# Loads of x in five pieces, new batch order and filler counts at both ends of attention, and an earlier weight split in the experts

## The chip, the core and the metric

The kernel runs on one core of one Trainium2 chip. The metric is the device time of one execution in microseconds (us); lower is better. Three executions of the kernel before took 906.54, 910.2 and 913.91 us, so the median is 910.2 us.

## What is computed

Two layers, each an attention over a context and then a mixture of experts, on x of 8 batches of 256 tokens of width 256, all in float32:

```python
x = x + tanh(g_xattn[0]) * L0_xattn(layernorm(x), ctx, ctx, ...)   # 16 heads of 16, softmax, output projection
x = x + tanh(g_ffn[0])   * L0_ffn(layernorm(x), ...)               # 8 experts, top 2, gelu, 256 -> 1024 -> 256, biases
x = x + tanh(g_xattn[1]) * L1_xattn(layernorm(x), ctx, mask, ...)  # the same shape, no mask applied
x = x + tanh(g_ffn[1])   * L1_ffn(layernorm(x), ...)               # top 2 of 8 by softmax; 7 experts with relu and a
                                                                   # capacity of 256 tokens each, the 8th passes x on
```

## The kernel before

The program is six phases, one after the other, with all engines meeting between them: attention, routing and experts of layer 0 (called L0), then the same of layer 1 (L1). The engines are named as in the profile: PE (TensorE), DVE (VectorE), ACT (ScalarE), POOL (GpSimd), SP (the queue that issues most DMAs). Within a phase each engine runs a list of steps written out by hand, and semaphores tie the lists together. A step that waits holds up everything behind it on its engine.

**Attention.** The unit is a batch b of 256 tokens. In float32 every projection is three matmuls of split operands: an operand is kept as a rounded high part (made by ACT for weights and x, by POOL for the context) and a low part (made by DVE, `weight_low`, `inputs_low`; for the context by POOL). A batch goes through `moments` and `normalise_rows` (layernorm; the two small steps between them, `rows_scale`, are POOL's), `x_transpose`, `queries`, `keys` and `values` on PE into one shared PSUM bank `ps_lin`, then eight `head_scores` whose row maxima DVE takes (`take_maxima`, 16 halves a batch), `max_transpose`, copies of queries, keys and maxima into slots by small DMAs on SP (`queries_to_slots`, `keys_to_slots`, `maxima_to_slots`), four chunks of `scores`, exponentials on ACT (`probabilities`) and `weigh_values`, `turn_heads`, `o_transpose`, `out_project`, and at last the layernorm and logits for the router. Batches overlap: a loop over b = 1 to 4 holds the steady state, and the first and last batches have lists of their own. `values(0)` needs `wv` split, and the bank `ps_lin` emptied by `keys(0)`. POOL also writes ones into `v` (`value_ones`), which `values(0)` waits for on DVE.

x is loaded by two DMAs, the first batch alone and then the other seven together, behind all four weights, and the wait for the second stands in `moments(1)`:

```python
def moments(b):
    if b < 2:
        dve.wait_ge(x_ld[b], 16)
```

**Fillers.** `fill_first(n)` and `fill_last(n)` are n transposes of the identity into a PSUM bank that nothing reads. They stand in PE's list where PE is expected to wait. Before the change there are 62 of them at the start of an attention phase and 42 at its end, in each layer.

**Experts.** The unit is a block of 256 gathered tokens with the weights of one expert: 23 blocks in L0, 7 in L1. PE runs `first_product(b + 1)` and then `second_product(b)`. The first product of a block needs its tokens turned (`turn`), split into high (`inputs_high` on ACT) and low (`inputs_low` on DVE), and its first weights split (`w1_high` on ACT, `w1_low` on DVE). For block b + 1 this is done among the four steps (jp = 0 to 3) in which ACT applies the activation of block b (`hidden`) and DVE splits the result (`hidden_parts`). `second_product` fills both halves (q = 0, 1) of one PSUM bank; DVE takes it out (`output`), in L0 ACT weighs it (`weigh`), and POOL adds it to the tokens in DRAM with two indirect DMAs (`add_to_tokens`), which first wait until those of the block before have landed:

```python
pool.wait_ge(y_ready, b + 1)
if b:
    pool.wait_ge(y_out[(b - 1) % 2], loaded(b - 1, QT))
```

## Time and profile before

| | |
|---|---|
| median of three runs | 910.2 us |
| lowest, highest | 906.54, 913.91 us |
| the profiled execution: its own time | 913.08 us |
| its span, from the first to the last instruction | 911.3 us |
| PE, DVE, ACT, POOL busy in the span | 791.0, 634.0, 467.3, 396.3 us |
| granted TensorE clock, mean | 0.901 |

The profiled execution took 2.9 us more than the median, and 1.8 us of its time lie outside the span. Times in the rows are microseconds from the start of the span unless marked ns. L0 attention runs from 4.2 to about 235 us, its experts from about 260 to 547; L1 attention from about 552 to 777, its experts from about 805 to the end.

### The profile page before, as it was taken

The numbers are of one execution on the slowest core, as the hardware profiler recorded it, in microseconds if no ns is written. First come the engines' busy times: TensorE is split into PE (matmuls) and PEld (weight loads), VectorE is DVE, ScalarE is ACT, GpSimd is POOL, SyncE is SP. The second block draws the span as 40 slices with busy tenths as digits, with TensorE's granted clock in tenths as the row PEclk, the third lists the DMA queues.
The fourth block names the chain that finished last, engine by engine and source line by source line (L and its number), as shares of the span: only waits on it lengthen the run. The fifth ranks groups of instructions, "written<-read, shape, count | busy, mean of one in ns | idle before, by whom it ended". The sixth has DMA issues, their size and how long they took to land. (4 is left out here: it accounts for less than half of the span.)

```text
span 911.3 us, 17723 instructions
## 1 busy us (share of the span) xinstructions
PE 791.0 (87%) x6936; PEld 662.9 (73%) x6936; DVE 634.0 (70%) x1207; ACT 467.3 (51%) x696; POOL 396.3 (43%) x374
## 2 busy tenths in 40 slices
PE   5889999998438999999999975999999998348995
PEld 5566677656338999999999974666676656338995
DVE  3667776642658999999999932677776743758882
ACT  3256666444036766666667632166666542335540
POOL 4534453110134677777777443544543110232652
PEclk9779999888859999999999997699999988658998
DMA  7112111021166777887777527112111020775742
GB/s 218 37 37 60 51 50 44 8 74 39 49 235 241 220 243 236 242 237 240 238 240 239 139 30 209 40 38 62 51 51 40 13 83 25 203 185 195 231 85 32
DMA packets 57139, 113.74 MB, mean 125 GB/s; under 512 B 14176, under 2 KB 43360, under 8 KB 49376
## 3 DMA queue, kind: packets, MB, share of 16 engines
q0 software_dynamic: 20256, 69.43, 27.1%
q1 hardware_dynamic: 36800, 43.18, 15.6%
q8 instruction: 55, 0.90, 0.4%
q14 instruction: 28, 0.23, 0.1%
HBM read 85.17 MB, written 18.75 MB: 114 GB/s over the span
## 5 line engine op out<-in xcount | busy, mean ns | idle before, releaser
L563 DVE TENSOR_REDUCE mx_a<-ps_max_a 128x2 f32<-128x512 f32 x256 | 164.4, 685 | 67.8 <-PE ps_max_a L826 65.3
L73 PE MATMUL ps_h_e<-xe_t_e,w_e 128*128 128x256 f32 x480 | 141.3, 294 | 9.7 <-DVE xe_t_e L1659 9.7
L435 ACT ACTIVATE prob_a<-ps_st_a 128x2048 f32<-128x2048 f32 x64 | 120.1, 1876 | 54.8 <-PE ps_st_a L846 45.4
L75 PE MATMUL ps_h_e<-xe_t_e,w_e 128*128 128x256 f32 x480 | 138.0, 287 | 0.0
L74 PE MATMUL ps_h_e<-xe_t_e,w_e 128*128 128x256 f32 x480 | 138.0, 287 | 0.0
L73 PE MATMUL ps_y_e<-w_e,h_e 128*128 128x256 f32 x480 | 132.8, 277 | 0.0
L75 PE MATMUL ps_y_e<-w_e,h_e 128*128 128x256 f32 x480 | 132.7, 276 | 0.0
L74 PE MATMUL ps_y_e<-w_e,h_e 128*128 128x256 f32 x480 | 132.7, 276 | 0.0
L73 PEld LDWEIGHTS ps_h_e<-xe_t_e,w_e 128*128 128x128 f32 x480 | 95.6, 199 | 10.9 <-DVE xe_t_e L1659 10.9
L1503 POOL DMA_INDIRECT xe_e<-normalised_weighted,token_of x60 | 78.5, 1309 | 46.8 <-POOLq L61 19.8
L312 POOL TENSOR_SCALAR r_var_eps_a<-r_mean_var_a 128x2 f32<-128x2 f32 x16 | 3.7, 229 | 216.3 <-DVE r_mean_var_a L590 216.3
L74 PEld LDWEIGHTS ps_h_e<-xe_t_e,w_e 128*128 128x128 f32 x480 | 94.3, 196 | 0.0
L75 PEld LDWEIGHTS ps_h_e<-xe_t_e,w_e 128*128 128x128 f32 x480 | 93.9, 196 | 0.0
L1525 POOL DMA_INDIRECT x<-y_e,token_of x46 | 78.5, 1706 | 34.2 <-ACT y_e L1579 18.6
L75 PEld LDWEIGHTS ps_y_e<-w_e,h_e 128*128 128x128 f32 x480 | 90.1, 188 | 0.0
L73 PEld LDWEIGHTS ps_y_e<-w_e,h_e 128*128 128x128 f32 x480 | 90.1, 188 | 0.0
L74 PEld LDWEIGHTS ps_y_e<-w_e,h_e 128*128 128x128 f32 x480 | 90.1, 188 | 0.0
L846 PE MATMUL ps_st_a<-q_s_a,k_s_a 17*128 17x256 f32 x1024 | 84.1, 424 | 4.9 <-DMA q_s_a<-m_t_a 4.3
L1634 DVE TENSOR_TENSOR h_e<-hid_e,h_e 128x512 fp32r<-128x512 f32 x120 | 84.2, 702 | 4.1
L826 PE MATMUL ps_max_a<-k_r_a,q_r_a 32*128 32x512 f32 x256 | 81.6, 561 | 4.1 <-DVE mx_a L563 1.9
L1570 ACT ACTIVATE hid_e<-ps_h_e,b_e 128x256 f32<-128x256 f32 x184 | 77.5, 482 | 6.8 <-PE ps_h_e L75 6.8
L1552 ACT ACTIVATE w_e<-w_raw_w 128x1024 fp32r<-128x1024 f32 x60 | 64.4, 1076 | 28.9 <-PEq L61 28.9
(210 smaller groups left out, 1746.8 us busy)
## 6 DMA issues: line engine op xcount, KB each, us to landing
w_raw_w<-L_w SPq DMA_DIRECT2D x14, 1024.0 KB
ctx_raw_a<-ctx_t SPq DMA_DIRECT2D x16, 256.0 KB, 5.3
k_s_a<-k_c_a SPq DMA_DIRECT2D x128, 32.0 KB, 2.0
q_s_a<-q_c_a SPq DMA_DIRECT2D x128, 32.0 KB, 2.0
normalised_weighted<-xr SPq DMA_DIRECT2D x16, 256.0 KB, 2.3
x_sb<-x SPq DMA_DIRECT2D x2, 1792.0 KB
x<-x_sb SPq DMA_DIRECT2D x8, 256.0 KB, 2.5
out<-x_sb SPq DMA_DIRECT2D x8, 256.0 KB, 2.5
```

Source lines behind the costliest of these rows:

```text
L73: pe.matmul(out, lhs[0], rhs[0], start=start, stop=False)
L74: pe.matmul(out, lhs[1], rhs[0], start=False, stop=False)
L75: return pe.matmul(out, lhs[0], rhs[1], start=False, stop=stop)
L435: act.activation(prob[n % 2][:, :, :, :], ps_st[:, :, :, :], ACT.Exp, scale=HD ** -0.5).then_inc(prob_ready, 1)
L563: dve.tensor_reduce(mx[:, q, h + 2 * j:h + 2 * j + 2], ps_max[j][:, :, :], AX.X, ALU.max).then_inc(max_done, 1)
L826: pe.matmul(ps_max[j][:, :, :], q_r[b % 2][r:r + 32, c, q * P:(q + 1) * P], k_r[b % 2][r:r + 32, c, :, :], start=True, stop=True).then_inc ...
L846: ins = pe.matmul(ps_st[:, g, kt, :], k_s[b % 3][rows, c, kt * P:(kt + 1) * P], q_s[b % 3][rows, c, :], start=True, stop=True)
L1503: pool.indirect_dma_start(out=xe[b % 2][:, q, :], out_offset=None, in_=dram["xw"], in_offset=bass.IndirectOffsetOnAxis(ap=shared["token_of ...
L1525: pool.indirect_dma_start(out=dram["out" if layer else "x1"], out_offset=bass.IndirectOffsetOnAxis(ap=shared["token_of"][:, t:t + 1], axis=0),
L1552: act.activation(w1[b % 2][0][:, k, :, :], w1_raw[b % 2][:, k * F:(k + 1) * F].rearrange("p (j f) -> p j f", j=FC), ACT.Copy).then_inc(w1_ ...
L1570: ins = act.activation(hid[jp % 2][:, j, :], ps_h[jp % RB][:, j, :], ACT.Gelu, bias=b1[b % 2][:, 2 * jp + j:2 * jp + j + 1])
L1634: dve.tensor_tensor(h[b % 2][1][:, js, :], hid[jp % 2][:, :, :], h[b % 2][0][:, js, :].bitcast(F32), ALU.subtract).then_inc(h_ready, 1)
```

## The change

Attention: x comes in five DMAs (batches 0 to 3 one each, then batches 4 to 7 together), set among the weights and context on SP's queue; `moments(b)` waits for its own piece. The order of the steps of the first and last batches is changed on all engines, and the filler counts rise from 62 to 86 at the start and from 42 to 75 at the end, in each layer. Experts: the first weights of blocks 0 and 1 are both split ahead of `inputs_high(0)` and `inputs_low(0)`; block 1's tokens are turned after the first quarter of `first_product(0)` and not the third, and split at jp = 1 and not 3; an unused Gelu on ACT in L0 stands ahead of the first block; and in the last block each half goes out by itself, the second half in the other PSUM bank.

```diff
@@ -222,19 +223,31 @@
                     sp.dma_start(q_s[b % 3][HD:P:32, c, :], m_t[c * HG:c * HG + HG, :]).then_inc(m_ld, 16)
 
             src = (dram["x1"][0:N, :] if layer else dram["x"]).rearrange("(t p) d -> p t d", p=P)
-            sp.dma_start(x[:, 0:QT, :], src[:, 0:QT, :]).then_inc(x_ld[0], 16)
-            sp.dma_start(w_raw["wq"][:, :, :], w3["wq"]).then_inc(wq_ld, 16)
+
+            def load_x(i):
+                tiles = slice(i * QT, i * QT + QT) if i < XP - 1 else slice(i * QT, TT)
+                sp.dma_start(x[:, tiles, :], src[:, tiles, :]).then_inc(x_ld[i], 16)
+
+            def load_weight(n, done):
+                sp.dma_start(w_raw[n][:, :, :], w3[n]).then_inc(done, 16)
+
+            load_x(0)
+            load_weight("wq", wq_ld)
             sp.dma_start(bq[:, :], dram["bq"]).then_inc(wq_ld, 16)
             load_context(0)
-            sp.dma_start(w_raw["wk"][:, :, :], w3["wk"]).then_inc(wk_ld, 16)
+            load_weight("wk", wk_ld)
             sp.dma_start(bk[:, :], dram["bk"]).then_inc(wk_ld, 16)
-            sp.dma_start(w_raw["wv"][:, :, :], w3["wv"]).then_inc(wv_ld, 16)
+            load_x(1)
+            load_weight("wv", wv_ld)
             sp.dma_start(bv[:, :], dram["bv"]).then_inc(wv_ld, 16)
+            load_context(1)
+            load_x(2)
             sp.dma_start(bo[:, :], dram["bo"]).then_inc(wo_ld, 16)
-            sp.dma_start(w_raw["wo"][:, :, :], w3["wo"]).then_inc(wo_ld, 16)
-            sp.dma_start(x[:, QT:TT, :], src[:, QT:TT, :]).then_inc(x_ld[1], 16)
-            for b in range(1, CB):
-                load_context(b)
+            load_weight("wo", wo_ld)
+            load_context(2)
+            load_x(3)
+            load_context(3)
+            load_x(4)
             sp.dma_start(gate_w[:, :, :], dram["gate_w"].rearrange("(k p) e -> p k e", p=P)).then_inc(gate_ld, 16)
             if layer:
                 sp.dma_start(gate_b[:, :], dram["gate_b"]).then_inc(gate_ld, 16)
...
@@ -625,12 +638,13 @@
             moments(0)
             normalise_rows(0)
             weight_low("wq")
+            weight_low("wk")
             inputs_low(0)
-            weight_low("wk")
             moments(1)
+            moments(2)
+            normalise_rows(1)
...
@@ -894,36 +907,36 @@
             def fill_last(n):
                 keep_busy(pe, ps_max[1][:, 0, 0:P], ident, n)
 
-            fill_first(31)
+            fill_first(24)
             x_transpose(0)
-            fill_first(7)
+            fill_first(12)
             queries(0)
-            fill_first(4)
+            fill_first(8)
             keys(0)
-            fill_first(4)
+            fill_first(8)
             values(0)
             head_scores(0, 0)
-            fill_first(1)
+            fill_first(3)
...
+            fill_last(2)
             router_turn(B - 2)
             weigh_values(B - 1, 3)
             router_logits(B - 2)
             turn_heads(B - 1, 1)
-            fill_last(3)
+            fill_last(6)
             o_transpose(B - 1)
-            fill_last(7)
+            fill_last(12)
             out_project(B - 1)
-            fill_last(19)
+            fill_last(31)
             router_turn(B - 1)
-            fill_last(3)
+            fill_last(6)
...
@@ -1515,13 +1531,16 @@
                     gather_weights(pool, "w2", buffers, shared, dram, b)
 
             def add_to_tokens(b):
-                pool.wait_ge(y_ready, b + 1)
+                if b < blocks - 1:
+                    pool.wait_ge(y_ready, b + 1)
                 if b:
                     pool.wait_ge(y_out[(b - 1) % 2], loaded(b - 1, QT))
                 elif layer:
                     pool.wait_ge(buffers["out_added"], 16 * (TT // CT))
                 for q in range(QT):
                     t = b * QT + q
+                    if b == blocks - 1:
+                        pool.wait_ge(last_ready, q + 1)
                     pool.indirect_dma_start(
                         out=dram["out" if layer else "x1"], out_offset=bass.IndirectOffsetOnAxis(ap=shared["token_of"][:, t:t + 1], axis=0),
                         in_=y[b % 2][:, q, :], in_offset=None, compute_op=ALU.add).then_inc(y_out[b % 2], 16)
...
@@ -1572,28 +1591,39 @@
                     ins.then_inc(hid_ready, 1)
 
             def weigh(b):
-                act.wait_ge(y_biased, b + 1)
+                if b < blocks - 1:
+                    act.wait_ge(y_biased, b + 1)
                 if b >= 2:
                     act.wait_ge(y_out[b % 2], loaded(b - 2, QT))
                 for q in range(QT):
+                    if b == blocks - 1:
+                        act.wait_ge(last_biased, q + 1)
                     ins = act.activation(y[b % 2][:, q, :], y_raw[b % 2][:, q, :], ACT.Copy, scale=slot_weight[:, b, q:q + 1])
-                ins.then_inc(y_ready, 1)
+                    if b == blocks - 1:
+                        ins.then_inc(last_ready, 1)
+                if b < blocks - 1:
+                    ins.then_inc(y_ready, 1)
 
             def inputs_high(b):
                 act.wait_ge(xe_ps, b + 1)
                 act.activation(xe_t[b % 2][0][:, :, :], ps_x[b % 2][:, :, :], ACT.Copy).then_inc(xe_hi, 1)
 
-            for k in range(KC):
-                w1_high(0, k)
+
+
+            for b in range(2):
+                for k in range(KC):
+                    w1_high(b, k)
+            if layer == 0:
+                act.activation(unread[:, :], shared["tanh_g"][:, 0:1], ACT.Gelu)
             inputs_high(0)
             for b in range(blocks):
                 for jp in range(NP):
                     if jp < KC:
-                        if b + 1 < blocks:
+                        if b and b + 1 < blocks:
                             w1_high(b + 1, jp)
                     else:
                         w2_high(b, jp - KC)
-                    if jp == NP - 1 and b + 1 < blocks:
+                    if jp == (NP - 1 if b else 1) and b + 1 < blocks:
                         inputs_high(b + 1)
                     if layer == 0 and jp == 0 and b >= 2:
                         weigh(b - 2)
...
@@ -1647,6 +1680,20 @@
                     dve.tensor_tensor(y_raw[b % 2][:, :, :], ps_y[b % 2][:, :, :], spread(b2[b % 2][:, :], 1, QT),
                                       ALU.add).then_inc(y_biased, 1)
 
+            def last_output(b):
+
+                if layer:
+                    dve.wait_ge(y_out[b % 2], loaded(b - 2, QT))
+                else:
+                    dve.wait_ge(y_ready, b - 1)
+                for q in range(QT):
+                    dve.wait_ge(last_ps, q + 1)
+                    if layer:
+                        dve.tensor_scalar(y[b % 2][:, q, :], ps_y[(b + q) % 2][:, q, :], slot_weight[:, b, q:q + 1], None,
+                                          ALU.mult).then_inc(last_ready, 1)
+                    else:
+                        dve.tensor_tensor(y_raw[b % 2][:, q, :], ps_y[(b + q) % 2][:, q, :], b2[b % 2][:, :], ALU.add).then_inc(last_biased, 1)
+
             def inputs_low(b):
                 dve.wait_ge(xe_hi, b + 1)
                 if layer:
...
@@ -1659,17 +1706,18 @@
                 dve.tensor_tensor(xe_t[b % 2][1][:, :, :], ps_x[b % 2][:, :, :], xe_t[b % 2][0][:, :, :].bitcast(F32),
                                   ALU.subtract).then_inc(xe_ready, 1)
 
-            for k in range(KC):
-                w1_low(0, k)
+            for b in range(2):
+                for k in range(KC):
+                    w1_low(b, k)
             inputs_low(0)
             for b in range(blocks):
                 for jp in range(NP):
                     if jp < KC:
-                        if b + 1 < blocks:
+                        if b and b + 1 < blocks:
                             w1_low(b + 1, jp)
                     else:
                         w2_low(b, jp - KC)
-                    if jp == NP - 1 and b + 1 < blocks:
+                    if jp == (NP - 1 if b else 1) and b + 1 < blocks:
                         inputs_low(b + 1)
                     hidden_parts(b, jp)
                 if b:
...
@@ -1697,7 +1745,7 @@
                             ins = split_matmul(pe, ps_h[jp % RB][:, j, :], [w1[b % 2][s][:, k, 2 * jp + j, :] for s in range(2)],
                                                [xe_t[b % 2][s][:, k, :] for s in range(2)], k == 0, k == KC - 1)
                     ins.then_inc(h_ps, 1)
-                    if jp == NP - 2 and b + 1 < blocks:
+                    if jp == (NP - 2 if b else 0) and b + 1 < blocks:
                         turn(b + 1)
 
             def second_product(b):
@@ -1705,10 +1753,18 @@
                 pe.wait_ge(h_ready, (b + 1) * NP)
                 wait(pe, y_ready if layer else y_biased, b - 1)
                 for q in range(QT):
+
+                    bank = ps_y[b % 2]
+                    if b == blocks - 1 and q:
+                        wait(pe, y_ready if layer else y_biased, b)
+                        bank = ps_y[(b + 1) % 2]
                     for j in range(FC):
-                        ins = split_matmul(pe, ps_y[b % 2][:, q, :], [h[b % 2][s][:, j, q * P:(q + 1) * P] for s in range(2)],
+                        ins = split_matmul(pe, bank[:, q, :], [h[b % 2][s][:, j, q * P:(q + 1) * P] for s in range(2)],
                                            [w2[b % 2][s][:, j, :] for s in range(2)], j == 0, j == FC - 1)
-                ins.then_inc(y_ps, 1)
+                    if b == blocks - 1:
+                        ins.then_inc(last_ps, 1)
+                if b < blocks - 1:
+                    ins.then_inc(y_ps, 1)
 
             turn(0)
             first_product(0)
```

Where the moved steps land, from the lists of instructions of both kernels. DVE, L0 attention, first batches, before (rows L612 split weights, L536 and L539 are `moments`, L545 is `normalise_rows`, L616 `inputs_low`, L554 `values`, L563 `take_maxima`):

```order
L545 TENSOR_SCALAR xn_a<-x_sb,mean_var_a,rstd_a 128x256 x2
L612 TENSOR_TENSOR wq_lo_a<-wq_raw_a,wq_hi_a 128x512
L616 TENSOR_TENSOR xn_t_lo_a<-ps_lin_a,xn_t_hi_a 128x512
L612 TENSOR_TENSOR wk_lo_a<-wk_raw_a,wk_hi_a 128x512
L536 BN_STATS stats_a<-x_sb 128x6 x2
L539 BN_AGGR mean_var_a<-stats_a 128x2 x2
L612 TENSOR_TENSOR wv_lo_a<-wv_raw_a,wv_hi_a 128x512
L545 TENSOR_SCALAR xn_a<-x_sb,mean_var_a,rstd_a 128x256 x2
L536 BN_STATS stats_a<-x_sb 128x6 x2
L539 BN_AGGR mean_var_a<-stats_a 128x2 x2
L554 TENSOR_TENSOR v_a<-ps_lin_a,bv_a 128x32x16
```

The same place after (L625, L549 and L552, L558, L629, L567):

```order
L558 TENSOR_SCALAR xn_a<-x_sb,mean_var_a,rstd_a 128x256 x2
L625 TENSOR_TENSOR wq_lo_a<-wq_raw_a,wq_hi_a 128x512
L625 TENSOR_TENSOR wk_lo_a<-wk_raw_a,wk_hi_a 128x512
L629 TENSOR_TENSOR xn_t_lo_a<-ps_lin_a,xn_t_hi_a 128x512
L549 BN_STATS stats_a<-x_sb 128x6 x2
L552 BN_AGGR mean_var_a<-stats_a 128x2 x2
L549 BN_STATS stats_a<-x_sb 128x6 x2
L552 BN_AGGR mean_var_a<-stats_a 128x2 x2
L558 TENSOR_SCALAR xn_a<-x_sb,mean_var_a,rstd_a 128x256 x2
L625 TENSOR_TENSOR wv_lo_a<-wv_raw_a,wv_hi_a 128x512
L549 BN_STATS stats_a<-x_sb 128x6 x2
L552 BN_AGGR mean_var_a<-stats_a 128x2 x2
```

Three `moments` now stand ahead of `values(0)`, for batches 1 to 3, where two stood, and the low part of `wv` waits behind batches 1 and 2.

POOL, start of L0 attention, before (L341 `key_ones`, L293 and L295 `rows_scale`, L329 and L331 `split_context`, L336 `round_queries`, L346 `value_ones`):

```order
L341 MEMSET k_s_a 128x1024 x3
L293 TENSOR_SCALAR var_eps_a<-mean_var_a 128x2
L295 TENSOR_TENSOR rstd_a<-var_eps_a,minus_half_a 128x2
L329 CAST ctx_t_hi_a<-ctx_raw_a 128x512
L331 TENSOR_TENSOR ctx_t_lo_a<-ctx_raw_a,ctx_t_hi_a 128x512
L293 TENSOR_SCALAR var_eps_a<-mean_var_a 128x2
L295 TENSOR_TENSOR rstd_a<-var_eps_a,minus_half_a 128x2
L336 CAST q_r_a<-q_c_a 128x512
L346 MEMSET v_a 128x32x16 x3
```

and after (L354, L306 and L308, L359, L342 and L344):

```order
L354 MEMSET k_s_a 128x1024 x3
L306 TENSOR_SCALAR var_eps_a<-mean_var_a 128x2
L308 TENSOR_TENSOR rstd_a<-var_eps_a,minus_half_a 128x2
L359 MEMSET v_a 128x32x16 x3
L342 CAST ctx_t_hi_a<-ctx_raw_a 128x512
L344 TENSOR_TENSOR ctx_t_lo_a<-ctx_raw_a,ctx_t_hi_a 128x512
```

The three memsets of `v` move up, to right behind the `rstd` that DVE's first `normalise_rows` waits for.

DVE, start of L0's experts, before (`w1_01` is the low part of block 0's first weights, `w1_11` that of block 1, `xe_t01` and `xe_t11` the low parts of their tokens, `h` the hidden parts):

```order
L1609 TENSOR_TENSOR w1_01_e0<-w1_raw0_w0,w1_00_e0 128x1024 x2
L1614 COPY b1_0_e0<-w1_raw0_w0 128x8
L1655 TENSOR_TENSOR by_expert_e0<-xe0_e0,block_is_w0 128x16
L1658 TENSOR_REDUCE slot_weight_e0<-by_expert_e0 128x2
L1659 TENSOR_TENSOR xe_t01_e0<-ps_x0_e0,xe_t00_e0 128x512
L1609 TENSOR_TENSOR w1_11_e0<-w1_raw1_w0,w1_10_e0 128x1024
L1632 CAST h00_e0<-hid0_e0 128x512
L1634 TENSOR_TENSOR h01_e0<-hid0_e0,h00_e0 128x512
L1609 TENSOR_TENSOR w1_11_e0<-w1_raw1_w0,w1_10_e0 128x1024
L1614 COPY b1_1_e0<-w1_raw1_w0 128x8
```

and after:

```order
L1639 TENSOR_TENSOR w1_01_e0<-w1_raw0_w0,w1_00_e0 128x1024 x2
L1644 COPY b1_0_e0<-w1_raw0_w0 128x8
L1639 TENSOR_TENSOR w1_11_e0<-w1_raw1_w0,w1_10_e0 128x1024 x2
L1644 COPY b1_1_e0<-w1_raw1_w0 128x8
L1702 TENSOR_TENSOR by_expert_e0<-xe0_e0,block_is_w0 128x16
L1705 TENSOR_REDUCE slot_weight_e0<-by_expert_e0 128x2
L1706 TENSOR_TENSOR xe_t01_e0<-ps_x0_e0,xe_t00_e0 128x512
L1662 CAST h00_e0<-hid0_e0 128x512
L1664 TENSOR_TENSOR h01_e0<-hid0_e0,h00_e0 128x512
L1702 TENSOR_TENSOR by_expert_e0<-xe1_e0,block_is_w0 128x16
L1705 TENSOR_REDUCE slot_weight_e0<-by_expert_e0 128x2
L1706 TENSOR_TENSOR xe_t11_e0<-ps_x1_e0,xe_t10_e0 128x512
```

Both halves of `w1_11` move ahead of block 0's tokens, and the low part of block 1's tokens comes right behind the first hidden part.

## Rows read from the trace of the kernel before

**Rows 1.** The page, granted TensorE clock in 40 slices of 22.8 us, in tenths.

```profile
PEclk9779999888859999999999997699999988658998
```

**Rows 2.** Timeline of PE, start of L0 attention: start, us, instruction, count, wait before.

```profile
20.13 0.39 PE L73 MATMUL ps_lin_a<-wv_hi_a,ctx_t_hi_a 128*128 128x256 f32 x1 [3.23 <-DVE wv_lo_a L612]
...
43.51 0.50 PE L826 MATMUL ps_max_a<-k_r_a,q_r_a 32*128 32x512 f32 x2 [0.34 <-ACT m_t_a L423]
...
66.27 0.50 PE L826 MATMUL ps_max_a<-k_r_a,q_r_a 32*128 32x512 f32 x2
```

**Rows 3.** Timeline of DVE, start of L0 attention.

```profile
9.09 0.73 DVE L545 TENSOR_SCALAR xn_a<-x_sb,mean_var_a,rstd_a 128x256 f32<-128x256 f32 x2 [1.17 <-POOL rstd_a L295]
...
18.46 0.76 DVE L536 BATCH_NORM_STATS2 stats_a<-x_sb 128x6 f32<-128x256 f32 x2 [5.24 <-DMA x_sb<-x]
...
21.00 2.68 DVE L545 TENSOR_SCALAR xn_a<-x_sb,mean_var_a,rstd_a 128x256 f32<-128x256 f32 x2 [0.93 <-POOL rstd_a L295]
...
36.01 2.57 DVE L563 TENSOR_REDUCE mx_a<-ps_max_a 128x2 f32<-128x512 f32 x4 [1.24 <-PE ps_max_a L826]
```

**Rows 4.** Timelines of ACT and of POOL, start of L0 attention.

```profile
11.34 0.63 ACT L447 ACTIVATE wv_hi_a<-wv_raw_a 128x512 fp32r<-128x512 f32 x1 [0.17 <-DMA bv_a<-L_bv]
...
16.55 0.84 ACT L389 ACTIVATE k_c_a<-ps_lin_a,bk_a 128x256 f32<-128x256 f32 x2 [1.91 <-PE ps_lin_a L75]
...
9.62 0.67 POOL L329 CAST ctx_t_hi_a<-ctx_raw_a 128x512 fp32r<-128x512 f32 x1 [0.57 <-DMA ctx_raw_a<-ctx_t]
...
21.48 1.45 POOL L346 MEMSET v_a<- 128x512 f32 x3
```

**Rows 5.** Busy time in two stretches, L0 attention: each engine's us, then PEclk.

```profile
20.60:34.20 13.60, 11.96 (x45) 8.44 (x44) 9.86 (x17) 0.99 (x2) 12.34 (x16) 0.50 0.21 53
...
47.90:58.20 10.30, 10.30 (x66) 6.86 (x62) 4.42 (x10) 3.75 (x2) 7.01 (x8) 0.50 0.23 51
```

**Rows 6.** Timeline of PE, start of L1 attention, the same three steps.

```profile
568.99 0.58 PE L73 MATMUL ps_lin_a<-wv_hi_a,ctx_t_hi_a 128*128 128x256 f32 x1 [4.40 <-DVE wv_lo_a L612]
...
594.00 0.49 PE L826 MATMUL ps_max_a<-k_r_a,q_r_a 32*128 32x512 f32 x2 [0.34 <-ACT m_t_a L423]
...
611.62 0.49 PE L826 MATMUL ps_max_a<-k_r_a,q_r_a 32*128 32x512 f32 x2
```

**Rows 7.** Busy time while PE runs only the 31 fillers of L1.

```profile
551.80:556.50 4.70, 4.67 (x22) 4.70 (x23) 1.00 (x4) 0.63 (x1) 3.53 (x6) 0.50 0.69 204
556.50:557.57 1.07, 1.07 (x12) 0.94 (x10) 0.80 (x3) 0.00 (x0) 0.24 (x1) 1.00 0.97 325
```

**Rows 8.** PE's timeline at block 1's first product, L0 and L1; busy time there.

```profile
279.65 0.38 PE L73 MATMUL ps_h_e<-xe_t_e,w_e 128*128 128x256 f32 x1 [3.16 <-DVE xe_t_e L1659]
...
823.90 0.58 PE L73 MATMUL ps_h_e<-xe_t_e,w_e 128*128 128x256 f32 x1 [3.35 <-DVE xe_t_e L1659]
...
279.65:285.60 5.95, 5.95 (x37) 5.95 (x38) 4.77 (x8) 3.07 (x6) 2.66 (x3) 0.71 0.66 244
297.05:303.00 5.95, 5.95 (x55) 5.95 (x54) 5.85 (x11) 4.95 (x9) 2.81 (x2) 1.00 0.76 148
...
823.90:832.70 8.80, 8.80 (x53) 8.80 (x54) 6.95 (x10) 4.82 (x7) 2.44 (x2) 0.68 0.63 211
```

**Rows 9.** Timeline of DVE, L0's experts: block 0's tokens, block 1's tokens.

```profile
266.58 0.18 DVE L1655 TENSOR_TENSOR by_expert_e<-xe_e,block_is_w 128x16 f32<-128x16 f32 x1 [3.26 <-ACT xe_t_e L1584]
...
278.92 0.68 DVE L1659 TENSOR_TENSOR xe_t_e<-ps_x_e,xe_t_e 128x512 fp32r<-128x512 f32 x1
```

**Rows 10.** Timelines of DVE and POOL at the end of the program.

```profile
901.43 0.88 DVE L1643 TENSOR_SCALAR y_e<-ps_y_e,slot_weight_e 128x256 f32<-128x256 f32 x2 [4.78 <-PE ps_y_e L75]
...
903.35 1.55 POOL L1525 DMA_INDIRECT out<-y_e,token_of  x1 [3.01 <-DMA out<-y_e,token_of]
```

**Rows 11.** PE at the end of L0 attention; busy time in a stretch there.

```profile
232.02 0.66 PE L729 MATMUL ps_lin_a<-ident,xr 128*128 128x128 f32 x4 [1.73 <-DVE xr L596]
...
208.00:219.00 11.00, 10.52 (x90) 6.61 (x88) 3.38 (x9) 4.33 (x5) 0.92 (x2) 0.69 0.01 1
```

131 lines of the change are left out of this document (67 added, 64 removed).

## Prediction

> **What bounds the kernel now.** I read the page first: PE is busy 791.0 of 911.3 us, so the time is PE's work plus PE's waits plus what a low TensorE clock stretches. The clock row [rows 1] tells where that is: a tenth of 9 means full speed (2.4 GHz), and the slices below it lie at the start and end of both attention phases and in routing and the first expert blocks after each, never in the steady middle. The change touches just these ends. So I read PE's timeline there, for each wait what released it, and busy time by stretch for the granted clock.
>
> At the start of attention PE waits 3.23 us in L0 and 4.40 us in L1 for the low part of `wv` [rows 2, 6]. DVE made that late not for want of weights: ACT had the high part of `wv` at 11.34 [rows 4], but in front of the low part stands `moments(1)`, which waits for the seven batches of x in one DMA and starts at 18.46 after 5.24 us of idling [rows 3]. After this wait PE's clock lies at 0.50 from 20.6 to 34.2, and again from 47.9 to 58.2 [rows 5]. At the start of the experts PE waits 3.16 us (L0) and 3.35 us (L1) for the low part of block 1's tokens [rows 8], which DVE reaches last in its list, at 278.92 [rows 9]; behind both waits the clock falls too. In a steady expert block PE has no wait, and DVE is close behind it: busy 5.85 of 5.95 us [rows 8].
>
> **Loads of x.** Removed: the wait on 1792 KB. Batch 1's piece is 256 KB and stands just ahead of `wv`, whose high part ACT starts at 11.34, so it should be there at about that time, against 18.46. Added: three more DMAs on SP of about 0.45 us of issue each, 1.4 us in all; what is queued behind them (the first slot copies) is wanted some 20 us later, and that hides them. `moments(2)` and `moments(3)` now stand ahead of `values(0)` on DVE. The pieces are 8.5 and 12 quarters of a megabyte into the queue; from the 5.5 that had landed at 11.34 to the 14 landed at 18.46 the queue moved 1.2 a us, so they land at about 14 and 17 us, ahead of need. What is late next is the bank: `keys(0)` is emptied at 16.55 + 0.84 = 17.39 [rows 4], and 0.4 us later `values(0)` can run, at 17.8 instead of 20.13. That is 2.3 us in L0, and 4.40 - 0.9 = 3.5 us in L1 by the same leftover.
>
> **POOL's memsets.** `value_ones` moves to just behind the `rstd` that frees DVE's first `normalise_rows`. The same DVE step took 0.73 us with POOL waiting, and 2.68 us with a POOL cast, the 1.45 us of memsets and another cast going on [rows 3, 4]. So 0 to 1.95 us is added in front of the whole chain of each layer. I take 1.0, since only the memsets and not the first cast coincide. The Trainium skill ("SBUF — State Buffer", Who interferes with whom) has one port pair shared by VectorE and GpSimd, taken for a whole instruction, so that the loser blocks and doesn't slow down. By that rule all of the memset time would be lost where it comes first, 1.45 us a layer and not 1.0.
>
> Net of this the first term is 2.3 - 1.0 = 1.3 us in L0 and 3.5 - 1.0 = 2.5 us in L1.
>
> **The clock behind it, and the fillers.** From `values(0)` to the first `head_scores` of batch 1 it takes 43.51 - 20.13 = 23.4 us in L0 and 594.00 - 568.99 = 25.0 us in L1 [rows 2, 6], mostly at low clock. What it takes at full clock I add up from DVE, which must do eight pairs of maxima at 1.29 us [2.57 for two pairs, rows 3] = 10.3; PE products between them that leave DVE idle, three of 1.24 [rows 3] = 3.7; the low part and the values taken out, 1.3; the first product and its way out 2.3; the turned maxima 1.0. That is 18.6, so 4.8 us less in L0 and 6.4 us in L1. The bounds are 0 (the clock falls all the same) and 6.8 (half of 13.6 us, if PE alone set the pace).
>
> From there to the loop L0 takes 66.27 - 43.51 = 22.8 us with 10.3 us at low clock, and L1 611.62 - 594.00 = 17.6 us with the clock up: L0 gives 5.1 us more if its clock holds, L1 nothing.
>
> Do fillers hold a clock? In L1 PE ran 31 fillers alone; its clock went from 0.50 to 1.00 among them, and they shrank from 0.21 us each to half [rows 7]. The Trainium skill ("TensorE: Matmul & The Clock Gate", Part 4) says transposes in PE's transpose mode don't engage the full clock and don't count as busy in the same way. By that the added fillers would be idle time, the clock would fall as before, and the sum would be the first rival's; this trace speaks against it.
>
> The fillers are a cost where PE would not have waited: 24 more at the start and 33 more at the end in each layer, 114 in all, 12 us at full clock. Behind the last `out_project` 12 more stand where PE waited 1.73 us after the old 19 [rows 11], and 12 x 0.11 = 1.3 us fit. At the start they follow longer waits. I count them at nothing, covered; without cover they cost the 12 us. One risk is mine to price: 31 fillers become 24 at the very start, and with the memsets a gap of some 3 us opens before `x_transpose(0)`. For this and other falls that stay I take 3.4 us off over the two layers.
>
> Attention's starts: 1.3 + 4.8 + 5.1 in L0, 2.5 + 6.4 in L1, less 3.4, is 16.7 us.
>
> **The ends of attention.** Steps change places by one or two, and PE is busy 10.52 of 11.00 us at a clock of 0.69 [rows 11]. If that rose to 1.00 it would be worth 3.4 us a layer; new orders may as well cost a wait of 1 or 2. I take 1 us for both layers, bounds -4 to +7.
>
> **The experts' start.** DVE idles 3.26 us before block 0's tokens [rows 9]; two pieces of `w1_low` (1.2 us each) fit there, so block 0 starts as before. ACT's two pieces and the table load for Gelu lie in the same idle time. The wait of 3.16 us goes, and the first product behind it runs at full clock: (1 - 0.71) x 5.95 = 1.7 us in L0; 3.35 and (1 - 0.68) x 8.80 = 2.8 us in L1 [rows 8]. Next late is DVE at block 2: its work per block nearly fills PE's time [rows 8], so PE, 3 us earlier, catches up with it. I take 1.0 off in L0, where DVE also copies biases and picks weights, and 0.5 in L1; bounds 0 and the whole wait. That is 3.9 + 5.6 = 9.5 us.
>
> **The last block.** Halving its output brings nothing. In L1 the result is out on DVE at 901.43 + 0.88 = 902.31, but POOL issues only at 903.35, released by the landing of the block before's DMAs [rows 10]. The new code waits for the same landing. In L0 the order is the same. 0 us, at most 0.5.
>
> **Sum.** 16.7 + 1 + 9.5 = 27.2 us less. The profiled execution of 913.1 would become 885.9; against the median of 910.2, 2.9 lower, that is 883.0. I forecast **883 us**.
>
> **Rivals.** (1) *The clock falls all the same.* PE still has steps with few rows or columns between fillers, and 47.9 to 58.2 was at 0.50 with PE busy in all of it [rows 5]. Then only 1.3 + 2.5 of the start and the experts' 9.5 stay: 13.3 us, 897. For it: that row. Against it: the fall at 20.6 follows a plain wait. (2) *DVE takes the wait over* in the experts: PE waits at block 2 for what it no longer waits for at block 1, and 7 us of 9.5 go, 890. For it: 5.85 of 5.95 us busy. Against it: DVE has 1.3 us less to do between the first hidden part and block 2. (3) *x is no earlier*: all loads share one queue, `moments(2)` or `moments(3)` waits in place of `moments(1)`. Then the start gives little and the experts stay, 900. For it: that three `moments` now precede `values(0)`. Against it: the rate above. (4) *Slower: fillers without cover.* If the clock is low when they run they take 0.21 us each [rows 7], 114 of them 24 us, against the 13.3 us saved in rival 1: 911 + 10 = 921. It decides from the point at which over half of the new ones are uncovered at low clock. For it: PE busy 10.30 of 10.30 us in one stretch [rows 5]. Against it: most stand before a step with a wait in the rows.
>
> **Chances.** Forecast 0.67, its own range 873 to 892; clock 0.17; DVE 0.08; x late 0.03; slower 0.05. The range is to leave out 2 in 10 or fewer: from 872 (ends of attention and clocks at their good bounds) to 899, which takes in rivals 1 and 2. About 1% is what a measurement of this kernel can tell from no change, 901 to 919. Below 901 lie the forecast, DVE, four fifths of the clock's case and half of the third, 0.89; within 1% 0.06; slower 0.05.
>
> **What would show it.** In the profile after: `moments(1)` on DVE near 12 us, `values(0)` near 18 to 19, the first `normalise_rows` at 0.7 (no lock) or about 2 us, the clock near 1.00 up to the loop, the first `head_scores` of batch 1 near 37 and of batch 2 near 55 us; in the experts no wait before block 1's first product, perhaps 1 us before block 2's; the end 15 us after the last matmul of the last block but one, as before. I am wrong if the clock row keeps its low slices, or if the waits of POOL or SP move into PE's list of the last batches.

## The result and the profile after

The changed kernel takes 897.64 us (median of 14 runs, 893.34 to 905.43) against 908.37 us (14 runs, 898.70 to 913.91): ratio 0.9899, 95% interval 0.9874 to 0.9923. It is 1.0% faster, the forecast was 3%. The forecast of 883 us was 14.6 us too low. The profiled execution took 899.82 us with a span of 898.1 us and a mean granted clock of 0.92, against 913.08, 911.3 and 0.90.

The page after, clock row, answers to [rows 1]:

```profile
PEclk9999899869859999999999997998999879659999
```

The second and third slices (L0's start) are 9 where 7 stood, and so is the 26th (L1's start), which was 6. Five figures are worse than before. The 8 in slice 5 (L0) and the 8 in slice 28 (L1), both 9 before, are the first sign of what went wrong; the 6 in slice 9 (8 before) and the 8 and 7 in slices 32 and 33 (9 and 8 before) lie at the ends of the two attentions.

The start of L0 attention after: PE's timeline (`values(0)`, first `head_scores` of batch 1, `scores(0, 0)`, first `head_scores` of batch 2), then DVE's, then POOL's. They answer to [rows 2, 3, 4]:

```profile
19.92 0.36 PE L73 MATMUL ps_lin_a<-wv_hi_a,ctx_t_hi_a 128*128 128x256 f32 x1 [0.21 <-ACT k_c_a L402]
...
38.41 0.49 PE L839 MATMUL ps_max_a<-k_r_a,q_r_a 32*128 32x512 f32 x2
...
42.20 1.10 PE L859 MATMUL ps_st_a<-q_s_a,k_s_a 17*128 17x256 f32 x13 [1.26 <-DMA q_s_a<-m_t_a]
...
57.25 0.58 PE L839 MATMUL ps_max_a<-k_r_a,q_r_a 32*128 32x512 f32 x2
```

```profile
9.26 2.13 DVE L558 TENSOR_SCALAR xn_a<-x_sb,mean_var_a,rstd_a 128x256 f32<-128x256 f32 x2 [1.17 <-POOL rstd_a L308]
...
11.91 1.76 DVE L625 TENSOR_TENSOR wk_lo_a<-wk_raw_a,wk_hi_a 128x512 fp32r<-128x512 f32 x1
13.60 0.68 DVE L629 TENSOR_TENSOR xn_t_lo_a<-ps_lin_a,xn_t_hi_a 128x512 fp32r<-128x512 f32 x1
14.20 0.74 DVE L549 BATCH_NORM_STATS2 stats_a<-x_sb 128x6 f32<-128x256 f32 x2
...
17.58 0.69 DVE L625 TENSOR_TENSOR wv_lo_a<-wv_raw_a,wv_hi_a 128x512 fp32r<-128x512 f32 x1 [0.47 <-ACT wv_hi_a L460]
```

```profile
9.19 1.44 POOL L359 MEMSET v_a<- 128x512 f32 x3
...
11.32 1.80 POOL L344 TENSOR_TENSOR ctx_t_lo_a<-ctx_raw_a,ctx_t_hi_a 128x512 fp32r<-128x512 f32 x1
```

`moments(1)` runs at 14.20 and waits for no load, and the first products of batches 1 and 2 stand at 38.41 and 57.25, where [rows 2] had 43.51 and 66.27: 9.0 us gained (37 and 55 were forecast, 38.4 and 57.3 came). The first line on DVE shows the price of the memsets: 2.13 us in place of 0.73. A second price stands below it: the low part of `wk`, now ahead of the low part of the tokens, took 1.76 us beside POOL's step of 1.80. So `values(0)` came only at 19.92, 0.2 us earlier than before, where 18 to 19 was forecast; nearly all of L0's 9.0 us were won behind it. In L1 `values(0)` stands 15.5 us behind the phase's first filler (558.89 less 543.37), where it stood 17.2: 1.6 us.

Then the gain goes. PE's timeline at `scores(2, 0)` of L0, and SP's queue between the maxima of batch 1 and those of batch 2 in the changed kernel:

```profile
86.85 1.15 PE L859 MATMUL ps_st_a<-q_s_a,k_s_a 17*128 17x256 f32 x16 [3.24 <-DMA q_s_a<-m_t_a]
```

```profile
56.98 2.20 SPq L223 DMA_DIRECT2D q_s_a<-m_t_a  x4
59.22 5.30 SPq L207 DMA_DIRECT2D q_s_a<-q_c_a  x8
64.58 5.09 SPq L207 DMA_DIRECT2D k_s_a<-k_c_a  x8
69.72 0.58 SPq L201 DMA_DIRECT2D ctx_raw_a<-ctx_t  x1
70.41 6.43 SPq L207 DMA_DIRECT2D q_s_a<-q_c_a  x8
76.89 5.73 SPq L207 DMA_DIRECT2D k_s_a<-k_c_a  x8
82.66 0.58 SPq L201 DMA_DIRECT2D ctx_raw_a<-ctx_t  x1
83.29 2.20 SPq L223 DMA_DIRECT2D q_s_a<-m_t_a  x4
```

The same queue in the kernel before:

```profile
66.15 2.22 SPq L222 DMA_DIRECT2D q_s_a<-m_t_a  x4
68.41 5.35 SPq L206 DMA_DIRECT2D k_s_a<-k_c_a  x8
73.80 0.58 SPq L200 DMA_DIRECT2D ctx_raw_a<-ctx_t  x1
74.50 4.94 SPq L206 DMA_DIRECT2D q_s_a<-q_c_a  x8
79.48 5.76 SPq L206 DMA_DIRECT2D k_s_a<-k_c_a  x8
85.28 0.58 SPq L200 DMA_DIRECT2D ctx_raw_a<-ctx_t  x1
86.50 2.21 SPq L222 DMA_DIRECT2D q_s_a<-m_t_a  x4
```

Count the rows between the two `q_s_a<-m_t_a`, which are the copies of the maxima of batches 1 and 2. The change put the copies of batch 2's queries behind the maxima of batch 1, so four groups of eight copies stand there instead of three, each copy at some 0.65 us on SP. SP issues from 56.98 on without a gap: 26.3 us from one set of maxima to the next, where it took 20.35 before and PE's round (from one `max_transpose` to the next) takes 20.6. Batch 2's maxima had been turned at 76.75 and could go only at 83.29; PE waits 3.24 us, and the clock falls behind the wait (0.50 in the second stretch below). L1 has the same wait, 2.08 us at 622.71, and low clock from 624.1 to 630.9. Each wait, with half of the 6.8 us at low clock behind it, comes to about what its layer lost: 6.6 of 6.8 us in L0, 5.5 of 5.6 in L1.

Busy time in stretches of the changed kernel (length, then PE, PEld, DVE, ACT, POOL, then PEclk, DMA share, GB/s):

```profile
19.92:38.41 18.49, 17.65 (x109) 12.74 (x109) 12.66 (x20) 6.72 (x13) 12.94 (x15) 1.00 0.21 54
88.20:95.00 6.80, 6.80 (x34) 5.72 (x37) 2.17 (x6) 2.56 (x3) 1.14 (x1) 0.50 0.11 26
56.15:76.75 20.60, 20.32 (x211) 14.04 (x212) 15.05 (x29) 13.14 (x15) 7.06 (x8) 1.00 0.21 51
...
208.00:219.00 11.00, 11.00 (x128) 7.73 (x127) 3.94 (x12) 6.04 (x6) 0.95 (x2) 1.00 0.15 48
```

The first stretch, from `values(0)` to batch 1, is what [rows 5] had at half clock for 13.6 us: 18.49 us at 1.00, where I had added up 18.6. Behind it the clock was low once more, from 43.8 to 47.2, after a wait of 1.26 us at `scores(0, 0)` that the kernel before has too (1.35 us at 47.39). The third is the round in which SP falls behind. The fourth answers to [rows 11]: the clock there is now 1.00, but it was at 0.50 from 176.9 to 194.0 instead.

At the start of L1's experts a wait appears that was not there, in the middle of the first product of block 0 (first row: block 0's tokens; last: block 1's):

```profile
798.84 1.13 PE L1735 MATMUL ps_x_e<-ident,xe_e 128*128 128x128 f32 x4 [8.65 <-DMA xe_e<-normalised_weighted,token_of]
...
807.14 0.75 PE L1735 MATMUL ps_x_e<-ident,xe_e 128*128 128x128 f32 x4 [2.76 <-DMA xe_e<-normalised_weighted,token_of]
```

```profile
801.50:807.10 5.60, 2.88 (x12) 2.59 (x12) 1.12 (x2) 0.60 (x1) 1.89 (x2) 0.69 1.01 413
```

The wait answers to [rows 8], whose 3.35 us before block 1's first product are gone. The rows of block 1 are gathered by index; POOL issued the second at 799.51, and it landed some 7.6 us later while the DMA engines were busy all of the time (1.01). SP had sent three loads of 1024 KB of weights at 797.28, 797.66 and 799.55. In the kernel before the third of them went 10 us behind the first and not 2.3, and PE asked for block 1's rows only at 818.5.

The end of the program, DVE and POOL, answers to [rows 10]:

```profile
885.78 0.48 DVE L1692 TENSOR_SCALAR y_e<-ps_y_e,slot_weight_e 128x256 f32<-128x256 f32 x1 [2.02 <-PE ps_y_e L75]
...
888.53 0.48 DVE L1692 TENSOR_SCALAR y_e<-ps_y_e,slot_weight_e 128x256 f32<-128x256 f32 x1 [2.27 <-PE ps_y_e L75]
```

```profile
890.01 1.55 POOL L1544 DMA_INDIRECT out<-y_e,token_of  x1 [2.57 <-DMA out<-y_e,token_of]
```

The first half is ready at 886.26, and POOL still waits for the landing of the block before's DMAs, as forecast.

**Where the 13.2 us of the spans' difference are.** From where a step stands in both traces (before minus after, each as a gain within its stretch): start of L0 to batch 1's turned maxima +9.2; from there to batch 3's, -6.8; the end of L0 +2.3; its routing -0.2; L0's experts +3.9, last block included; start of L1 to batch 1's turned maxima +9.1; to batch 3's, -5.6; end of L1 and routing -0.5; L1's experts +1.5, end +0.3. These are two executions: the profiled one of the kernel before took 4.7 us more than the median of its 14, that of the changed kernel 2.2 us more. So the medians differ by 10.7 us, and single terms below a few us are uncertain.

### The profile page after: what moved, and what is told of

Read it like the earlier page. It is cut to its first block and busy times, and to the rows that moved or that the text cites. A ratio compares the mean times of both kernels' runs of the same rounds, so it can differ in the third digit from the quotient of the medians.

```text
span 898.1 us, 17965 instructions
## 1 busy us (share of the span) xinstructions
PE 794.1 (88%) x7050; PEld 669.3 (75%) x7050; DVE 633.6 (71%) x1208; ACT 468.2 (52%) x697; POOL 397.9 (44%) x374
## 5 line engine op out<-in xcount | busy, mean ns | idle before, releaser
L576 DVE TENSOR_REDUCE mx_a<-ps_max_a 128x2 f32<-128x512 f32 x256 | 164.4, 684 | 65.2 <-PE ps_max_a L839 62.6
L73 PE MATMUL ps_h_e<-xe_t_e,w_e 128*128 128x256 f32 x480 | 139.6, 291 | 4.7 <-DVE xe_t_e L1706 4.7
L75 PE MATMUL ps_h_e<-xe_t_e,w_e 128*128 128x256 f32 x480 | 136.5, 284 | 0.0
L74 PE MATMUL ps_h_e<-xe_t_e,w_e 128*128 128x256 f32 x480 | 136.4, 284 | 0.0
L1519 POOL DMA_INDIRECT xe_e<-normalised_weighted,token_of x60 | 79.0, 1317 | 43.8 <-POOLq L61 19.8
L73 PEld LDWEIGHTS ps_h_e<-xe_t_e,w_e 128*128 128x128 f32 x480 | 93.9, 196 | 5.7 <-DVE xe_t_e L1706 5.7
L74 PEld LDWEIGHTS ps_h_e<-xe_t_e,w_e 128*128 128x128 f32 x480 | 92.8, 193 | 0.0
L75 PEld LDWEIGHTS ps_h_e<-xe_t_e,w_e 128*128 128x128 f32 x480 | 92.5, 193 | 0.0
L839 PE MATMUL ps_max_a<-k_r_a,q_r_a 32*128 32x512 f32 x256 | 83.4, 560 | 2.0 <-DVE mx_a L576 0.8
```

Source lines behind the costliest of these rows:

```text
L73: pe.matmul(out, lhs[0], rhs[0], start=start, stop=False)
L74: pe.matmul(out, lhs[1], rhs[0], start=False, stop=False)
L75: return pe.matmul(out, lhs[0], rhs[1], start=False, stop=stop)
L576: dve.tensor_reduce(mx[:, q, h + 2 * j:h + 2 * j + 2], ps_max[j][:, :, :], AX.X, ALU.max).then_inc(max_done, 1)
L839: pe.matmul(ps_max[j][:, :, :], q_r[b % 2][r:r + 32, c, q * P:(q + 1) * P], k_r[b % 2][r:r + 32, c, :, :], start=True, stop=True).then_inc ...
L1519: pool.indirect_dma_start(out=xe[b % 2][:, q, :], out_offset=None, in_=dram["xw"], in_offset=bass.IndirectOffsetOnAxis(ap=shared["token_of ...
```

## The experiments

All times are medians (12 runs for old_experts, new_experts_alone and pieces_new_slots, 6 for the others behind the changed kernel). The kernel before had 908.3 us beside the first four, 908.2 beside the next four and 906.6 beside the last four; so a comparison across groups is off by up to 1.7 us. "Batch 1" and "batch 3" in the table are the start of `max_transpose` of that batch in the profile, "block 0" and "block 6" the start of the turn of that block's tokens in L1, all in us.

| kernel | time | ratio to before (95%) | L0 batch 1, 3 | L1 start | L1 batch 1, 3 | L1 block 0, 6 |
|---|---|---|---|---|---|---|
| before | 908.4 | 1 | 65.32, 107.45 | 551.83 | 610.68, 652.83 | 810.27, 876.96 |
| changed | 897.6 | 0.9899 (0.9874-0.9923) | 56.15, 105.07 | 543.37 | 593.16, 640.93 | 798.84, 864.07 |
| q2_first | 888.3 | 0.9781 (0.9725-0.9838) | 55.03, 101.56 | 538.96 | 588.80, 631.16 | 787.45, 853.00 |
| old_experts | 904.4 | 0.9963 (0.9930-0.9996) | 55.00, 103.63 | 544.89 | 594.77, 642.72 | 800.73, 867.57 |
| new_experts_alone | 901.9 | 0.9928 (0.9889-0.9967) | 60.88, 104.52 | 539.39 | 596.00, 638.11 | 795.58, 861.11 |
| old_fillers | 896.3 | 0.9881 (0.9823-0.9938) | 57.08, 102.67 | 540.14 | 589.46, 635.32 | 793.21, 858.80 |
| pieces_alone | 893.7 | 0.9851 (0.9803-0.9900) | 54.99, 97.10 | 541.68 | 593.12, 635.27 | 793.58, 857.97 |
| ones_late | 898.1 | 0.9892 (0.9851-0.9933) | 53.92, 102.20 | 538.33 | 589.06, 638.88 | 796.99, 862.49 |
| hold_weights | 895.6 | 0.9864 (0.9825-0.9904) | 60.09, 108.83 | 546.87 | 598.21, 644.54 | 798.80, 860.11 |
| q2_first_ctx_later | 885.6 | 0.9752 (0.9719-0.9785) | 54.69, 97.05 | 534.74 | 587.46, 629.84 | 788.05, 853.34 |
| pieces_new_slots | 904.2 | 0.9975 (0.9940-1.0010) | 55.28, 104.34 | 543.13 | 596.96, 641.59 | 802.28, 868.89 |
| pieces_experts_hold | 888.6 | 0.9788 (0.9726-0.9850) | 55.58, 97.69 | 539.39 | 592.19, 634.30 | 791.35, 852.72 |
| q2_ctx_hold | 882.5 | 0.9739 (0.9694-0.9784) | 57.69, 100.07 | 537.62 | 590.32, 632.68 | 790.47, 852.76 |
| all_four | 881.5 | 0.9718 (0.9672-0.9764) | 56.45, 98.91 | 537.20 | 585.33, 627.69 | 785.42, 848.54 |

Read the fourth column as a difference: two rounds of the loop take 42.1 us (before, pieces_alone), 48.9 in the changed kernel.

**SP's queue.** The expectations write q2 and k2 for the copies of batch 2's queries and keys, m2 for those of its maxima. q2_first:

```diff
+            queries_to_slots(2)
             maxima_to_slots(1)
-            queries_to_slots(2)
             keys_to_slots(2)
```

> The changed kernel with one step moved: SP copies the queries of batch 2 to their slots ahead of the maxima of batch 1, not behind. Theory (SP's queue): in the changed kernel the copies of q2, k2, q3 and k3, four times about 5 us, stand between the maxima of batch 1 and those of batch 2, SP issues without a gap from 57 to 90.6 us, and PE waits at 86.85 for the maxima of batch 2; q2 fits into the gap of SP before 57. Then that wait goes in both layers, batch 3's max_transpose comes about 6.5 us (L0) and 5.4 us (L1) earlier, and the time is 897.6 - 12 = 886 us (883 to 889). Rival (the clock): the low stretch at 88.2 to 95.0 us is what costs, and it comes for PE's light steps whatever SP does: within 2 us of 897.6. Rival (DMA): the maxima wait for the transfers themselves, not for their issue: then m2 lands hardly earlier, 894 to 898.

888.3 us, 9.4 below the changed kernel. The wait at `scores(2, 0)` is gone in both layers, and L1's two rounds take 42.4 us instead of 47.8. In L0 they take 46.5: SP issued the maxima of batch 1 1.5 us later than in the changed kernel. Timelines of SP and PE in q2_first:

```profile
52.25 6.17 SPq L207 DMA_DIRECT2D q_s_a<-q_c_a  x8
58.46 2.59 SPq L223 DMA_DIRECT2D q_s_a<-m_t_a  x4
```

```profile
62.48 0.91 PE L859 MATMUL ps_st_a<-q_s_a,k_s_a 17*128 17x256 f32 x9 [0.85 <-DMA q_s_a<-m_t_a]
```

A wait of 0.85 us, and from 63.2 to 70.0 the clock is at 0.50. q2_first_ctx_later takes this apart:

```diff
-            load_context(5)
             queries_to_slots(2)
             maxima_to_slots(1)
+            load_context(5)
```

> As q2_first, and the load of context block 5 moved behind the maxima of batch 1 on SP. In q2_first SP issued the maxima of batch 1 at 58.46 us instead of 56.98, PE waited 0.85 us at 62.48, and the clock was low from 63.2 to 70.0, in L0 alone. Theory (this wait comes from SP's queue, 0.63 us too long): the wait is 0.2 us or gone, the clock holds, 3 to 4 us in L0: 888.3 - 3.5 = 885. Rival (the clock falls there for PE's light work): 888.

885.6 us. The maxima go at 56.41, the wait is gone, the clock stays up, and the two rounds take 42.4 us in L0 as well:

```profile
51.35 5.02 SPq L207 DMA_DIRECT2D q_s_a<-q_c_a  x8
56.41 2.19 SPq L223 DMA_DIRECT2D q_s_a<-m_t_a  x4
59.02 0.39 SPq L201 DMA_DIRECT2D ctx_raw_a<-ctx_t  x1
```

The step of 2.7 us between these two medians is within their intervals; L0's 4.2 us are read from the traces.

**The loads by themselves.** pieces_alone is the kernel before with only the block of loads (and the waits of `moments`) of the change:

```diff
+            load_x(1)
...
-            sp.dma_start(x[:, QT:TT, :], src[:, QT:TT, :]).then_inc(x_ld[1], 16)
...
+            load_x(4)
...
-                if b < 2:
+                if b < XP:
                     dve.wait_ge(x_ld[b], 16)
```

> The kernel before with one part of the change alone: x comes in five pieces in the new order of loads; every list of steps, the fillers and the experts stay as before. Theory (the early load frees values(0), and the clock then holds by itself): values(0) near 18 us instead of 20.13, no low clock at 20.6 to 34.3, the first head_scores of batch 1 near 37 to 39 instead of 43.5, and most of the starts' gain of 9 us a layer is here without a new order or fillers: 908.4 - 16 = 892 (888 to 896). Rival (the new order of the steps brings it): values(0) at 18, but the clock falls behind another wait, 908.4 - 6 = 902 (899 to 906). Rival (the pieces themselves come no earlier than the one DMA): 908.

893.7 us: this one part gives 1.5%, at least as much as the whole change (the two intervals overlap). PE's timeline at `values(0)`, DVE's at `moments(1)`:

```profile
17.65 0.36 PE L73 MATMUL ps_lin_a<-wv_hi_a,ctx_t_hi_a 128*128 128x256 f32 x1 [0.64 <-ACT k_c_a L400]
```

```profile
14.56 0.74 DVE L547 BATCH_NORM_STATS2 stats_a<-x_sb 128x6 f32<-128x256 f32 x2
```

`values(0)` stands at 17.65 (17.8 forecast), released by `keys(0)`'s way out and no longer by `wv`. Batch 1's turned maxima come 10.3 us earlier in L0 and 7.4 in L1 (17.56 less the 10.15 by which L1 starts earlier): 17.7 us, with 62 fillers and the old order. The clock is not up all of the time: it is low from 24.2 to 27.6 in L0 and from 560.0 to 566.9 in L1, where it was low for 23.9 and 20.5 us before. Batch 1's first `head_scores` stands at 38.26, as in the changed kernel (38.41): there `values(0)` is 2.3 us later, and the stretch behind it shorter by as much. In that stretch of L0 the clock was 1.00 in all nine profiles with the new order of steps and fell in all three with the old order and x in pieces, so the new order, or what comes with it, does hold it there.

pieces_new_slots then adds to it SP's new order of the first slot copies and nothing else:

```diff
+            queries_to_slots(0)
             keys_to_slots(0)
             load_context(4)
-            queries_to_slots(0)
-            queries_to_slots(1)
             maxima_to_slots(0)
-            queries_to_slots(2)
+            queries_to_slots(1)
             keys_to_slots(1)
             load_context(5)
             maxima_to_slots(1)
+            queries_to_slots(2)
```

> The converse of q2_first: the kernel before with x in five pieces (pieces_alone, 893.7 us), and of all the new orders only that of SP's first copies to slots, q2 behind the maxima of batch 1. Theory (SP's queue alone takes back the gain): batch 3's max_transpose comes 6 to 8 us later than in pieces_alone in L0, 5 to 6 us in L1, with a wait of 2 to 3 us on the maxima of batch 2 before scores(2, 0), and the time is 893.7 + 11 = 905 us (901 to 908). Rival (the new orders of PE, DVE and ACT are needed for the loss too): 893 to 896.

904.2 us, 2.4 below its own kernel before: 12.1 of the 14.5 us go again, by the order of one queue. PE's timeline in L0:

```profile
84.92 2.09 PE L857 MATMUL ps_st_a<-q_s_a,k_s_a 17*128 17x256 f32 x16 [2.40 <-DMA q_s_a<-m_t_a]
```

The two rounds take 49.1 us. In L1 I missed: there is no such wait. The clock was low from 592.7 to 602.9 us, with PE busy in all of it; that a PE so slow lets SP keep up is my reading. What made the clock fall there, no row shows: the last wait before it was 0.18 us, and pieces_alone has the same without a fall. In this profile L1 still lost 4.9 us against pieces_alone, with 13.6 us more at low clock (that stretch and 572.2 to 575.6). So the mechanism is shown for L0 here, and for L1 by q2_first. This run moves the copies of q0 and of the first maxima too; that q2 alone does it is shown by q2_first.

**Fillers.** old_fillers has the changed kernel's order with the old counts:

```diff
-            fill_first(24)
+            fill_first(31)
...
-            fill_last(31)
+            fill_last(19)
```

> The changed kernel with the counts of fillers of the kernel before (31, 7, 4, 4, 1, 2, 3, 1, 2, 2, 3, 2 at the start, 3, 1, 3, 3, 0, 3, 7, 19, 3 at the end). Theory (fillers hold the clock): the clock falls behind the waits at the start, batch 1's first head_scores comes 2 to 5 us later than 38.4 in L0, and the time is 901 to 906. Rival (fillers are idle time to the clock, the earlier loads alone brought it): 896 to 899, the milestones of the start the same. Rival (uncovered fillers): the time falls, by up to 2 us at each end of attention, 893 to 896.

896.3 us: no difference that can be told. Busy time from `values(0)` to batch 1 there:

```profile
20.00:37.80 17.80, 15.96 (x90) 10.68 (x90) 12.40 (x20) 6.62 (x13) 12.59 (x15) 1.00 0.20 52
```

18 fillers fewer in the stretch, 1.7 us less PE work (17.65 against 15.96), and the clock is 1.00 all the same; the ends of attention stand as in the changed kernel to within the spread between profiles. Neither did the added fillers hold the clock, nor did they cost. A kernel without any fillers was not run.

**The memsets.** ones_late:

```diff
-            value_ones()
             split_context(0)
             rows_scale(1)
             round_queries(0)
+            value_ones()
```

> The changed kernel with POOL's memsets of value_ones back behind round_queries(0). Theory (the memsets lock DVE's first normalise_rows): this step takes 0.7 us again, the first x_transpose comes at 9.9 instead of 11.45 us, 1.6 us earlier in each layer, 897.6 - 3 = 894.6 us. Rival (what is late next is a load or DVE's low part of wk, so that the step's delay was hidden): batch 1's first head_scores stays at 38.4, 897 to 898. Rival (the memsets come late for the values and cost there): 898 to 900.

898.1 us, no difference. The lock is there, and it is gone:

```profile
9.22 0.73 DVE L558 TENSOR_SCALAR xn_a<-x_sb,mean_var_a,rstd_a 128x256 f32<-128x256 f32 x2 [1.17 <-POOL rstd_a L308]
...
11.33 1.59 DVE L625 TENSOR_TENSOR wk_lo_a<-wk_raw_a,wk_hi_a 128x512 fp32r<-128x512 f32 x1 [0.77 <-ACT wk_hi_a L460]
12.85 0.68 DVE L629 TENSOR_TENSOR xn_t_lo_a<-ps_lin_a,xn_t_hi_a 128x512 fp32r<-128x512 f32 x1
```

1.4 us are saved in the first row, and half of them go again: the low part of `wk`, which the change put ahead of the low part of the tokens, waits for ACT, so `queries(0)` runs at 13.67 instead of 14.42. Batch 1's first `head_scores` comes at 37.69, 0.7 us earlier. That its turned maxima come 2.2 us earlier (56.15 to 53.92) is for the rest the clock, which did not fall at 43.8 in this profile. At SP's queue, which this kernel still has, both end: batch 3 stands 48.3 us behind batch 1, with a wait of 2.65 us at 84.03.

**The experts.** old_experts and new_experts_alone exchange the whole expert phase (`expert_phase` of one kernel with the rest of the other; no shorter diff says it).

> The changed attention with the expert phase of the kernel before. By the two traces the experts gave 3.4 + 0.5 us in L0 and 1.5 + 0.3 us in L1 of the difference, so 897.6 + 5.7 = 903.3 us (901 to 906). Rival (the prediction's terms: experts 9.5 us, and the attention's loss hides it): 907. Rival (the new code of the last block costs something): 900 or less.

> The attention of the kernel before with the changed expert phase, the converse. If the parts add up: 908.4 - 5.7 = 902.7 us (900 to 905). By the prediction's 9.5 us: 899. In L1 the new wait of PE for the landed tokens of block 1 should be there too, since it comes from the expert phase alone, 2 to 3 us at its first product's second quarter.

904.4 and 901.9 us: the phase is worth 6.7 us in the one exchange and 6.5 in the other. L0 gives 3.9 or more every time: from block 0's turn to the start of L1, last block included, the old code takes 287.0 to 287.5 us (four profiles) and the new one 282.2 to 283.1. In L1 blocks 0 to 6 take 64.4 to 66.8 us with the old code (the same four) and 65.2 to 65.6 with the new (six): next to nothing. Some 1 to 2 us of the two exchanges' medians have no place in the traces and are within their intervals. The new wait is in new_experts_alone too, 2.85 us at 803.97. The single edits of the expert phase (early split, early turn, unused Gelu, last block) were not run apart.

new_experts_alone shows one thing more. Its attention is that of the kernel before, and yet batch 1's turned maxima come at 60.88 and not at 65.32: the clock falls behind `values(0)` (19.4 to 33.1), but the second fall of [rows 5], 47.9 to 58.2, is not there, though the wait before `scores(0, 0)` is (1.26 us at 47.56). Busy time:

```profile
40.00:61.00 21.00, 18.10 (x171) 12.10 (x170) 15.91 (x28) 12.39 (x17) 7.46 (x8) 1.00 0.19 46
```

So 4.4 of the 9.2 us that L0's start gained between the two profiles belong to a fall that the kernel before has in one profile and not in the other.

hold_weights takes away what I blamed for it, in L1:

```diff
+                sp.wait_ge(xe_ld[1], loaded(1, QT))
                 for b in range(blocks):
                     load_weights(b)
```

> The changed kernel, and in L1 SP holds its loads of expert weights (blocks 2 and 3) until block 1's tokens have landed. Theory (the gather of block 1 shares the DMA engines with 3 MB of weights): it lands 3 to 4 us earlier, near 802 to 803.5 us instead of 807.1, the wait of 2.76 us before block 1's turn goes, the clock does not fall at 808, and L1's experts gain 3 to 4.5 us: 893 to 895. Rival (the gather is slow by itself, 256 rows by index): the wait stays, 897 to 898. Rival (the weights held back are then late): a wait on weights before block 2, 898 to 902.

895.6 us. The median alone (2 us) would prove nothing; the trace does. Blocks 0 to 6 take 61.3 us, block 1's turn follows the product without a wait, and the clock doesn't fall at 808. Busy time in the first quarter of block 0's product, up to that turn, then SP's queue:

```profile
801.50:804.20 2.70, 2.70 (x13) 2.70 (x14) 0.00 (x0) 0.00 (x0) 1.89 (x2) 0.50 0.39 102
```

```profile
802.64 0.33 SPq L1500 DMA_DIRECT2D w_raw_w<-L_w  x1
803.01 0.43 SPq L1503 DMA_DIRECT2D w_raw_w<-L_w  x1
803.50 0.42 SPq L1500 DMA_DIRECT2D w_raw_w<-L_w  x1
```

SP was released at 802.64 by the landing of the rows that had come at about 807.1, with the gathers issued at the same times. The weights, 5 us later, are still in time. This profile's attention was 4 us slower in L0 (clock low at 43.3 to 53.6), which hides some of the gain in its span.

**Putting it together.**

> The changed kernel with q2's copies ahead of the maxima of batch 1, context block 5 behind them, and the weights of L1 held back until block 1's tokens landed. 885.6 - 3 = 882.6 us (880 to 886).

> The kernel q2_ctx_hold with two more steps put back in attention: POOL's value_ones behind round_queries(0), and the split of wk on ACT and DVE behind the tokens of batch 0. With value_ones alone back, queries(0) came at 13.67 us instead of 14.42, since DVE's low part of wk stood ahead of the low part of the tokens; with both back it should come at 12.2 us as in pieces_alone. Theory: 2.2 us earlier in each layer, of which values(0) and batch 1's first head_scores give on at least half: 882.6 - 3 = 880 us (877 to 883). Rival (the bank or DVE's maxima set the pace after values(0)): within 1.5 us of q2_ctx_hold.

> The kernel before with x in five pieces, the changed expert phase, and in it the weights of L1 held back until block 1's tokens landed; no new order of attention's steps and no new fillers. If the parts add up: 893.7 - 6 (experts, from the two runs that exchanged the phase) - 3 (weights held back) = 885 us (882 to 888). If the new orders of attention are worth something of their own, this stays behind the next kernel by that.

882.5, 881.5 and 888.6 us. The sums held but for the last, which is 3.6 us above its sum and 0.6 above its range. The kernel before was 1.7 us faster beside these three than beside the runs that the sums start from, so against it each saves 1.7 us less than the plain times say. all_four also puts the split of `wk` back on DVE and ACT:

```diff
-            weight_low("wk")
             inputs_low(0)
+            weight_low("wk")
```

It is the fastest kernel here, 2.8% below the one before; against q2_ctx_hold the difference of 1 us is not one, as the rival had it: `queries(0)` came at 12.20 as forecast and `values(0)` at 18.40, but the time hardly moved. pieces_experts_hold keeps all of attention's old orders and fillers and comes to within 7 us of all_four by the medians. Their intervals overlap, and its profile has the same span as that of q2_ctx_hold (886.7 us), so what the new orders of attention are worth with SP's queue mended stays open between 0 and 7 us.

## Why the prediction was wrong

- **Starts of attention, 16.7 us forecast:** right in the cause, the number in part by luck. 9.2 and 9.1 us up to batch 1, 18.2 together, and pieces_alone shows the cause: the load, and most of the low clock behind the wait. Term by term: `values(0)` 1.3 and 2.5 forecast, 0.2 and 1.6 measured; the stretch to batch 1, 4.8 and 6.4 forecast, 4.9 and 6.5 measured (the 18.6 us at full clock were 18.49); to batch 2, 5.1 and 0 forecast, 3.9 and 0.7 measured. The first term was too high because the order of `wk`'s low part had no price. The 3.4 us taken off for falls that stay covered the misses. The 5.1 us were priced from a fall that new_experts_alone, with the same attention, doesn't have.
- **The step that failed** is the one on SP: "what is queued behind them (the first slot copies) is wanted some 20 us later, and that hides them". It priced three added loads and not the moved copies, which were put at nothing without a count. The diff showed q2 going behind the maxima of batch 1; at eight copies of 0.63 us a batch and operand, the sum from one set of maxima to the next was 4 x 5 us and two context loads and the maxima's own 2.2, some 23.4 us, against a round of PE of 20.4 us; 26.3 us were measured, since some groups took over 5 us. So SP's queue was longer than the round. Measured: 6.8 and 5.6 us lost, 12.4 of the forecast's 27.2. The chain is shown from both sides: the order alone brings the loss (pieces_new_slots), and putting it back removes it (q2_first, q2_first_ctx_later). No rival named SP; the last sentence of the prediction did, but for the last batches.
- **Experts' start, 9.5 us forecast:** L0 3.9 forecast and 3.9 measured, and the wait on DVE before block 2's first product, put at 1.0, is there with 1.48 us (284.94). L1 5.6 forecast and about 1.5 measured (next to nothing against the spread). There too the next wait was put at block 2 on DVE; it came at block 1's turn, on a gather. The turn had moved ahead by 2.9 us (5.3 us behind block 0's turn in hold_weights, 8.2 before), and I had not asked whether the rows had landed by then. With the weights held back L1 gives 2 to 4 us more.
- **Memsets, 1.0 us a layer:** they took 1.4 us of DVE's step and 0.75 us of the path. The Trainium skill ("SBUF — State Buffer", Who interferes with whom) says that the loser of the shared port waits for the other's whole instruction; with 2.13 against 0.73 us beside memsets of 1.44 the trace agrees with that price for the step better than with my 1.0.
- **Fillers:** counted at nothing, rightly. But the reason was half wrong: that they carry the clock is not shown. With 62 or 86 of them it was 1.00 in the same stretch of the new order. The rival of uncovered fillers at low clock (921) had its price wrong as well, as they stand where PE would wait. The clock's rival (897) hit the number and not the mechanism: the stretch from `values(0)` ran at 1.00.
- **Ends of attention, 1 us forecast:** 2.3 in L0 and -0.5 in L1 between the two profiles, but from batch 3 to the experts' block 0 L0 took 151.7 to 158.8 us in five profiles with the old order and 153.7 to 156.1 in nine with the new one, so no gain is shown. **Last block:** at most 0.5 forecast, and 0.3 to 0.6 in the traces.
- **The base:** 910.2 us was the median of three; over 14 executions it is 908.4, from which the same sum gives 881.2.

With the terms as measured in the two profiles the sum is 27.2 + 1.5 (starts) - 12.4 (SP) - 4.1 (L1's experts) + 0.8 (ends) = 13.0 us; the spans differ by 13.2.

## What to carry to other kernels

A diff that moves a step moves each DMA that it issues: count what stands in the issuing queue between two transfers that others wait for, in time, and compare it with the round that you expect after the change, not the one before. When a step is put earlier, ask of every input whether it has landed by then and what else the DMA engines carry at that time. And test the parts alone: here one part gave at least as much as the whole change, and a second, a few moved lines of one queue, took most of it back.

## What the runs showed of the hardware

- Copies of few rows into slots cost SP 0.62 to 0.80 us each to issue (4.94 to 6.43 us for eight), and the DMA engines were far from busy meanwhile: a share of 0.21 in the round from 56.15 to 76.75.
- A wait of 0.85 us on PE was followed by 6.8 us at 1.2 GHz (q2_first, 63.2 to 70.0). Without it the clock stayed at 2.4 GHz there (q2_first_ctx_later). Not every such wait is followed by a fall: new_experts_alone has one of 1.26 us at 47.56 and holds 1.00 from 40 to 61 us.
- A DVE step of 0.73 us took 2.13 beside POOL's memsets of 1.44, and the split of `wk` 1.76 beside a POOL step of 1.80 where it took 0.69 in pieces_alone.
- The clock also falls with no wait over 0.2 us just before it: 592.7 to 602.9 us at 0.50 with PE busy in all of it (pieces_new_slots), and not in pieces_alone, which differs in SP's order alone. It makes single profiles of equal code differ by 2 to 4 us in a phase, so a phase was compared over several.
- A gather of rows by index landed 6.7 us after its issue had ended (800.46 to some 807.1) beside 3 MB of weights, and 2.2 us after it (800.43 to 802.64) with them held back.
